# A transformer written anew: joined value and output weights, four column groups, feed-forward between tiles

## Chip, cores and metric

The kernel runs on one core of one Trainium2 chip. The metric is the device time of one execution in microseconds (us), the median of three runs.

## What is computed

The input x has the shape (2, 1024, 128): two sequences of 1024 tokens with 128 features. Six blocks follow one another, each with a residual: a windowed transformer of six layers, a recurrence over the tokens, the same transformer again (with the same weights), a mixture of 20 experts, full attention, and the mixture again. The change touches the two passes of the transformer alone. One of its layers, cut to what matters:

```
x = attn_layer(shift_tokens(x)) + x     # the last 64 features are taken from the token before
x = ffn_layer(shift_tokens(x)) + x

def attn_layer(x):                      # 16 heads of 64, Wqkv is 128 x 3072, Wo is 1024 x 128
    q, k, v = split(x @ Wqkv)
    q = rotary(l2norm(q) * qs); k = rotary(l2norm(k) * ksc)
    # windows of 32 tokens; each sees itself and the window before it (64 keys, a band mask)
    attn = softmax(mask(8 * q @ k.T)); out = attn @ v
    return out @ Wo

def ffn_layer(x):                       # 341 hidden features
    a, gate = split((layernorm(x) * g + b_ln) @ W1 + b1)
    return (a * gelu(gate)) @ W2 + b2
```

## The kernel before

Everything is float32. The activations lie in SBUF with features on the partitions (`c.xA`, `c.xB`); a tile is 128 tokens of one sequence, so that a layer has 16 tiles. `transformer` normalises x, and then runs `layer_phase` six times in a loop of the hardware (`nc.Fori`). `layer_phase` holds the programs of the five engines, which meet only at semaphores. Its tiles go through a hand-written pipeline of four stages, one tile of each sequence in turn: `project` (Q and K projection, L451), `turn` (rotated and normalised Q and K transposed, L413), `attend` (scores, softmax, values), `finish` (output projection and residual). Two tiles are in the loop body of `run`; the first and last tiles stand outside it, and behind the last one come the four groups of the feed-forward, 512 tokens each (`FeedForward`), after which the next layer starts.

What each engine does for one tile:

- TensorE projects Q and K (4 matmuls of 512 columns, L451), projects V for each of the four windows with its 64 keys (2 matmuls of 512 columns, one for the even and one for the odd heads, which write to partitions 0 to 63 and 64 to 127, L475), transposes Q and K (16 transposes, L413), the probabilities (8, L484) and the output (8, L440), adds the mask and forms scores (64 matmuls of 64 columns that read 64 partitions, L431), multiplies probabilities and values (64 of the same shape, L400), and projects the output with Wo (8 matmuls, L459). A matmul in float32 is two instructions in the trace, a transpose is one.
- VectorE rotates Q and K (L515, L523), sums squares (L555), takes the reciprocal square root in twelve small steps (`rsqrt_steps`, L92 to L98), takes each head's maximum (L538), subtracts it (L543), sums the exponentials (L567), and scales the output by the reciprocal sum (L593).
- ScalarE squares (L634), takes one exponential over all 16 heads (L627), and copies from PSUM: Q and K (L669), values (L643), probabilities (L647), the turned output (L623). In the feed-forward it does the scaling (L871) and Gelu (L881). Each layer loads the table of Exp (L670) and that of Gelu (L650) once.
- GpSimd adds the two rotated products (L371), scales them by the norm (L376), and makes shifted copies of x (L349, L352).

The queue of SyncE loads the next layer's weights when the last tile of a layer is done. The order in each engine's queue is fixed by the text of `stages`; an instruction that waits holds up all that stand behind it on its engine.

## Time and profile before

| | us |
|---|---|
| median of three runs | 7947.51 (7939.41 to 7956.17) |
| span of the profiled execution | 7947.7 |
| first transformer, first table load to the addition of its result | 2265.8 |
| second transformer, the same | 2269.9 |
| one layer (second layer to third) | 378.37 |
| one tile in the middle of a layer | 19.72 |
| TensorE, VectorE, ScalarE, GpSimd busy over the span | 6508.3, 5680.7, 2813.2, 1991.7 |

The span runs from the first to the last instruction of one execution on the chip. "Busy" is the time in which an engine executes; a wait on a semaphore is idle time. The mean length of a matmul (mean ns) contains the time that it spends in the array, so starts matter more than lengths: from one start to the next the trace tells how fast TensorE goes. PEld is the loading of the stationary operand, which can run beside matmuls. A granted clock of 1.00 is 2.4 GHz, one of 0.50 is 1.2 GHz.

### The profile page before, as it was taken

The page shows a single profiled execution, that of the slowest core. Times are in us where ns is not written, and L with a number is a line of the kernel's source. Part 1 is how long each engine was busy: PE and PEld are TensorE (multiplying, and loading weights), DVE is VectorE, ACT ScalarE, POOL GpSimd, SP SyncE. Part 2 cuts the span into 40 slices and gives each one's busy share as a digit, 9 for nine tenths or more (in the row PEclk, how much of TensorE's full clock was granted, in tenths as well). Part 3 has the DMA queues.
Part 4 walks back from the last instruction along what each step waited for, and adds up shares of the span by engine and source line. Part 5 has one row for each costly group of instructions (what it writes and reads, how often), then busy time and mean ns, then how long its engine had stood idle before and what let it go on. Part 6 is the DMA issues. An engine that isn't in the chain of part 4 may idle for free. (4 is left out here: it accounts for less than half of the span.)

```text
span 7947.7 us, 238408 instructions
## 1 busy us (share of the span) xinstructions
PE 6508.3 (82%) x89716; PEld 4710.8 (59%) x89716; DVE 5680.7 (71%) x26551; ACT 2813.2 (35%) x7328; POOL 1991.7 (25%) x2075
## 2 busy tenths in 40 slices
PE   8999999999976666666666666679999999999887
PEld 5656656565656565655656565656565655656544
DVE  6676767676767777777777777777666676767566
ACT  4444444444432222222222222234444444444311
POOL 4343535353510000000000000034444353535200
PEclk9999999999975555555555555589999999999898
DMA  0000000000000000000000000000000000000000
GB/s 28 11 4 14 1 14 1 14 1 14 1 15 2 2 2 2 2 2 2 2 2 2 2 2 2 2 4 0 15 11 4 11 4 14 1 14 1 18 2 12
DMA packets 30765, 50.49 MB, mean 6 GB/s; under 512 B 2032, under 2 KB 25291, under 8 KB 28235
## 3 DMA queue, kind: packets, MB, share of 16 engines
q1 hardware_dynamic: 29614, 40.54, 1.6%
q8 instruction: 425, 6.96, 0.4%
q14 instruction: 314, 2.56, 0.1%
q10 hardware_dynamic: 412, 0.42, 0.0%
HBM read 39.91 MB, written 1.05 MB: 5 GB/s over the span
## 5 line engine op out<-in xcount | busy, mean ns | idle before, releaser
L1048 PE MATMUL g_bank<-hbuf,Wgates 128*128 128x2 f32 x2048 | 600.9, 363 | 1024.2 <-DVE hbuf L1136 970.3
L1048 PEld LDWEIGHTS g_bank<-hbuf,Wgates 128*128 128x128 f32 x2048 | 513.0, 311 | 1140.0 <-DVE hbuf L1136 1085.3
L1090 ACT ACTIVATE tg<-g_bank 128x2 f32<-128x2 f32 x1024 | 176.1, 172 | 1690.9 <-PE g_bank L1048 1690.9
L1156 POOL TENSOR_TENSOR xB<-hbuf,xA 128x32 f32 x64 | 16.4, 256 | 2853.0 <-DVE hbuf L1136 2853.0
L371 POOL TENSOR_TENSOR t1b<-t1b,t2b 128x1024 f32<-128x1024 f32 x192 | 451.7, 2354 | 687.1 <-DVE t2b L523 687.1
L371 POOL TENSOR_TENSOR t1a<-t1a,t2a 128x1024 f32<-128x1024 f32 x192 | 451.7, 2354 | 684.7 <-DVE t2a L523 684.7
L1060 PE MATMUL e_bank<-tg,Weg 128*128 128x2 f32 x2048 | 579.4, 352 | 0.0
L1032 PEld LDWEIGHTS s_bank<-hparts,Wparts 128*128 128x128 bf16 x12288 | 571.0, 117 | 0.0
L1110 DVE TENSOR_SCALAR sg<-es 128x4 f32<-128x4 f32 x1024 | 174.4, 170 | 554.5 <-ACT es L1092 554.5
L1060 PEld LDWEIGHTS e_bank<-tg,Weg 128*128 128x128 f32 x2048 | 515.1, 312 | 0.0
L1032 PE MATMUL s_bank<-hparts,Wparts 128*128 128x2 bf16 x12288 | 469.6, 165 | 0.0
L555 DVE TENSOR_REDUCE ssqb<-sqb 128x16 f32<-128x1024 f32 x192 | 232.7, 1215 | 187.5 <-ACT sqb L634 187.5
L376 POOL TENSOR_TENSOR t1b<-t1b,rnormb 128x1024 f32<-128x1024 f32 x192 | 361.1, 1902 | 11.6 <-DVE rnormb L98 11.6
L376 POOL TENSOR_TENSOR t1a<-t1a,rnorma 128x1024 f32<-128x1024 f32 x192 | 361.0, 1901 | 11.6 <-DVE rnorma L98 11.6
L555 DVE TENSOR_REDUCE ssqa<-sqa 128x16 f32<-128x1024 f32 x192 | 232.5, 1215 | 182.3 <-ACT sqa L634 182.3
L1127 DVE SCALAR_TENSOR_TENSOR no<-ex,iso,fno 128x1 f32<-128x1 f32 x2048 | 352.0, 213 | 3.6 <-issue 1.7
L1146 DVE SCALAR_TENSOR_TENSOR cn<-ex,sg,fcn 128x1 f32<-128x1 f32 x2048 | 351.8, 214 | 0.0
L431 PEld LDWEIGHTS banksa<-KT,QTa 64*32 64x32 f32 x12288 | 292.1, 107 | 41.0 <-issue 41.0
L431 PEld LDWEIGHTS banksb<-KT,QTb 64*32 64x32 f32 x12288 | 292.1, 107 | 40.7 <-issue 40.7
L643 ACT COPY Vwb<-banksb 128x512 f32<-128x512 f32 x384 | 224.8, 586 | 256.5 <-PE banksb L475 256.1
L643 ACT COPY Vwa<-banksa 128x512 f32<-128x512 f32 x384 | 224.7, 586 | 255.9 <-PE banksa L475 255.5
L431 PE MATMUL banksa<-KT,QTa 64*32 64x64 f32 x12288 | 308.3, 218 | 0.0
(435 smaller groups left out, 16401.7 us busy)
## 6 DMA issues: line engine op xcount, KB each, us to landing
Wqkv<-in_L_ffn_Wqkv SPq DMA_DIRECT2D x13, 1536.0 KB, 6.5
Wo<-in_L_ffn_Wo SPq DMA_DIRECT2D x13, 512.0 KB, 7.6
W<-in_L_ffn_W SPq DMA_DIRECT2D x12, 341.0 KB
W<-in_L_ffn_W SPq DMA_DIRECT2D x12, 128.0 KB
xt<-in_L_attn_x SPq DMA_DIRECT2D x2, 512.0 KB
rope<-in_rope SPq DMA_DIRECT2D x1, 1024.0 KB, 7.5
out<-ot SPq DMA_DIRECT2D x4, 256.0 KB
W<-in_L_ffn_W SPq DMA_DIRECT2D x12, 42.5 KB
```

The lines of the kernel that those rows point to most:

```text
L371: pool.tensor_tensor(t1[:, part], t1[:, part], t2[:, part], ALU.add).then_inc(s.rot_sum, 1)
L376: pool.tensor_tensor(qview(t1[:, part]), qview(t1[:, part]), c.rnorm[:, i * HEADS:(i + 1) * HEADS].unsqueeze(2).to_broadcast([P, HEADS, DH ...
L431: last = pe.matmul(sc[WIN * w:WIN * w + WIN, col:col + KEYS], c.QT[rows, pair, WIN * w:WIN * w + WIN], c.KT[b][rows, pair, WIN * w:WIN * w ...
L555: dve.tensor_reduce(c.ssq[:, i * HEADS:(i + 1) * HEADS], qview(sq[:, i * INNER:(i + 1) * INNER]), AX.X, ALU.add).then_inc(s.ssq_done, 1)
L643: act.copy(c.Vw[:, w, :], vo[:, bank * 512:(bank + 1) * 512]).then_inc(s.v_ready, 1)
L1032: last = pe.matmul(out, Wparts[:, gate, w_part, :], hparts[:, h_part, :], start=False, stop=(w_part, h_part) == LAST_TERM, skip_group_chec ...
L1048: pe.matmul(g_bank[j][:, s * B:(s + 1) * B], Wg[:, 3, 1, :], h, start=False, stop=True, skip_group_check=True).then_inc(g_done, 1)
L1060: pe.matmul(e_bank[j][:, s * B:(s + 1) * B], Weg[:, :], tg[:, :], start=False, stop=True, skip_group_check=True).then_inc(e_done, 1)
L1090: act.activation(tg[:, :], g_bank[j][:, s * B:(s + 1) * B], ACT.Tanh).then_inc(tg_ready, 1)
L1110: dve.tensor_scalar(sg[:, :, :], es[:, :, :], 1.0, None, ALU.add).then_inc(sg_done, 1)
L1127: last = dve.scalar_tensor_tensor(out=no[:, b:b + 1], in0=ex[:, b:b + 1], scalar=iso[:, b:b + 1], in1=fno[:, b:b + 1], op0=ALU.mult, op1=A ...
L1146: last = dve.scalar_tensor_tensor(out=cn[:, 1, b:b + 1], in0=ex[:, b:b + 1], scalar=sg[:, 0, b:b + 1], in1=fcn[:, 1, b:b + 1], op0=ALU.mul ...
```

## The change

`layer_phase` and `FeedForward` go. Each pass of the transformer becomes one straight program of 96 tiles (six layers of 16) and six further steps, without loops of the hardware. Tiles now run through one sequence and then the other. In step i the engines work on tile `new` = i (projection of Q, then of K), tile `now` = i-1 (transposes, scores, exponentials), tile `old` = i-2 (values, transposed probabilities) and tile `last` = i-3 (probabilities times values, residual). In it:

- Wv and Wo are multiplied once a layer, head by head, into a 128 x 128 matrix for each head (`turn_weights`, `join_weights`; `take_weights` and `keep_weights` copy them from PSUM). This is done in steps 6 to 11 of the layer before. Values then have 128 features for each head, the output projection and the transposes of the output go, and one transpose of 128 x 128 is left (`turn_output`).
- Values are formed once for each window of 32 tokens, by four matmuls of 512 columns with 32 stationary columns, to four groups of 32 partitions. The probabilities are laid out so that 4 heads of 32 keys fill the 128 partitions; `attend` has 32 matmuls of 128 columns.
- K is stored block-diagonally (`KT` holds two heads side by side, with zeros between them), so that 32 score matmuls of 128 columns that read all 128 partitions take the place of 64. ScalarE fills it in four copies, one for each half and parity (`take_k`); GpSimd moves the last window (`move_k`).
- The exponential is taken head by head: 16 ACTIVATEs of 64 columns, with the negated maximum as bias, each of which also gives its sum (`accum_out`). VectorE's subtraction and its sum go; it only inverts the sums, and GpSimd multiplies the probabilities by them (`norm_probs`, two instructions of 512 columns).
- The Q and K projections share two banks of PSUM, K's after Q's, and the scores, the turned Q and the turned K share two. Values, turned probabilities and the weight products share one bank (`vp`), each waiting until ScalarE has copied the one before.
- The feed-forward works on groups of two tiles (256 columns) and is spread over the steps: `rows` in an even step, `back` and `gates` with `gelu` in the odd one after it, `lins`, `multiply`, `contract` and `finish` in the next even one.
- The rotary tables of the next layer are multiplied by GpSimd in steps 8 to 11; weights have two buffers and are no longer loaded in `load_phase`. At the start GpSimd clears `KT` (2 x 2560 columns) and `Vw` (4096 columns).

VectorE's order in a step is: `rotate_q(new)`, `squares_q(new)`, `residual(last)`, in even steps `multiply`, then `rotate_k(new)`, `largest(now)`, in even steps `finish`, then `squares_k(new)`, `norms(new)`, `invert(now)`, and in even steps `normalise` (statistics, reciprocal square root and scaling of a group). GpSimd's is: `move_k(now)`, `add_q(new)`, in even steps `shift_rows`, then `shift(new + 1)`, `add_k(new)`, `norm_q(new)`, `norm_k(new)`, `norm_probs(now)`.

```diff
                 sp.dma_start(maskf[:, :, :], d["mask"]).then_inc(mask_in, 16)
                 sp.dma_start(c.rope[:, :, :, :], d["rope"]).then_inc(rest_in, 16)
-                sp.dma_start(c.Wqkv[:, :], d["L0_ffn_Wqkv"][0]).then_inc(rest_in, 16)
-                sp.dma_start(c.Wo[:, :, :], d["L0_ffn_Wo"][0].rearrange("(j p) n -> p j n", p=P)).then_inc(rest_in, 16)
-                sp.wait_ge(rest_in, 16 * 5)
+                sp.wait_ge(rest_in, 16 * 3)
...
-def layer_phase(nc, c, layer, nm):
...
-class FeedForward:
...
+def tensor_program(pe, c, s, N):
...
+    def project_q(n):
+        layer = tile_place(n)[0]
+        pe.wait_ge(s.weights_in[layer % 2], 16 * (layer // 2 + 1))
+        pe.wait_ge(s.xq_ready, 2 * n + 2)
+        if n:
+            pe.wait_ge(s.k_prod, 2 * n)
+        for h in range(2):
+            last = pe.matmul(qk[h], c.xq[n % 4][:, :], c.Wqk[layer % 2][:, h * 512:(h + 1) * 512], start=True, stop=True)
+        last.then_inc(s.q_done, 1)
...
+    def turn_q(n):
+        pe.wait_ge(s.q_scaled, n + 1)
+        if n:
+            pe.wait_ge(s.exp_done, n)
+        for half in range(2):
+            for k in range(half * HALF, (half + 1) * HALF):
+                last = pe.transpose(sc[:, k * P:(k + 1) * P], t1[:, k * P:(k + 1) * P], c.ident[:, :])
+            last.then_inc(s.q_turned, 1)
...
+    def score(n):
+        layer, b, t = tile_place(n)
+        pe.wait_ge(s.kt_ready, 4 * n + 4)
+        pe.wait_ge(s.k_moved, 2 * n + 2)
+        for h in range(2):
+            pe.matmul(sc[:, h * 512:(h + 1) * 512], c.identb[:, :], c.mask[:, t, :].unsqueeze(1).to_broadcast([P, 8, KEYS]),
+                      start=True, stop=False, skip_group_check=True)
+        for pair in range(PAIRS):
+            for w in range(NW):
+                last = pe.matmul(sc[WIN * w:WIN * w + WIN, pair * 2 * KEYS:(pair + 1) * 2 * KEYS],
+                                 c.QT[:, pair, WIN * w:WIN * w + WIN],
+                                 c.KT[n % 2][:, pair, :, WIN * w:WIN * w + KEYS],
+                                 start=False, stop=True, skip_group_check=True)
+        last.then_inc(s.scored, 1)
...
+    def values(n, w):
+        layer = tile_place(n)[0]
+        pe.wait_ge(s.wvo_ready, 4 * (layer + 1))
+        if w == 0 and n:
+            pe.wait_ge(s.v_ready, 4 * n)
+            before, j = divmod(n + 1, TILES)
+            if before + 1 < N // TILES and 6 <= j < 8:
+                pe.wait_ge(s.wv_ready, 2 * (before + 1) + j - 5)
+            if before + 1 < N // TILES and 8 <= j < 12:
+                pe.wait_ge(s.wvo_ready, 4 * (before + 1) + j - 7)
+        if w == 1 or w == 3:
+            pe.wait_ge(s.v_ready, 4 * n + w)
+        if w == 2:
+            pe.wait_ge(s.pt_ready, 2 * n + 2)
+        for hq in range(4):
+            last = pe.matmul(vp[WIN * hq:WIN * hq + WIN, :], c.xq[n % 4][:, WIN * w:WIN * w + WIN], c.Wvo[layer % 2][:, hq, :],
+                             start=True, stop=True)
+        last.then_inc(s.v_done, 1)
...
+    def turn_probs(n, pc):
+        pe.wait_ge(s.p_scaled, 2 * n + pc + 1)
+        if pc == 0:
+            pe.wait_ge(s.v_ready, 4 * n + 2)
+        else:
+            pe.wait_ge(s.pt_ready, 2 * n + 1)
+        for quad in range(QUADS):
+            last = pe.transpose(vp[:, quad * P:(quad + 1) * P], c.probs[n % 2][:, quad, pc, :, :].rearrange("p h j -> p (h j)"),
+                                c.ident[:, :])
+        last.then_inc(s.p_turned, 1)
...
+    def attend(n):
+        pe.wait_ge(s.v_ready, 4 * n + 4)
+        pe.wait_ge(s.pt_ready, 2 * n + 2)
+        if n:
+            pe.wait_ge(s.x_done, n)
+        first = NW * (n % 2)
+        for pc in range(2):
+            for quad in range(QUADS):
+                for w in range(NW):
+                    slot = (first + w - 1 + pc) % (2 * NW)
+                    last = pe.matmul(o[WIN * w:WIN * w + WIN, 0:P], c.PT[:, pc, quad * P + WIN * w:quad * P + WIN * w + WIN],
+                                     c.Vw[:, slot, quad * P:(quad + 1) * P],
+                                     start=(pc == 0 and quad == 0), stop=(pc == 1 and quad == QUADS - 1), skip_group_check=True)
+        last.then_inc(s.pv_done, 1)
...
+    for i in range(N + 6):
+        new, now, old, last = i, i - 1, i - 2, i - 3
+        even, g = i % 2 == 0, (i - 4) // 2
+        layer, j = divmod(i, TILES)
+        if new < N:
+            project_q(new)
+        if 0 <= now < N:
+            turn_q(now)
+        if 0 <= last < N:
+            attend(last)
+        if 0 <= old < N:
+            values(old, 0)
+        if 0 <= now < N:
+            turn_k(now)
+        if 0 <= last < N:
+            turn_output(last)
+        if 0 <= old < N:
+            values(old, 1)
+        if even and 0 <= g - 1 < G:
+            lins(g - 1)
+        if not even and 0 <= g < G:
+            back(g)
+        if new < N:
+            project_k(new)
+        if 0 <= old < N:
+            turn_probs(old, 0)
+        if 0 <= now < N:
+            score(now)
+        if 0 <= old < N:
+            turn_probs(old, 1)
+            values(old, 2)
+        if even and 0 <= g - 1 < G:
+            contract(g - 1)
+        if not even and 0 <= g < G:
+            gates(g)
+        if 0 <= old < N:
+            values(old, 3)
+        if even and 0 <= g < G:
+            rows(g)
+        if layer + 1 < N // TILES and 6 <= j < 12:
+            pe.wait_ge(s.v_ready, 4 * (old + 1))
+            if j < 8:
+                turn_weights(layer + 1, j - 6)
+            else:
+                join_weights(layer + 1, j - 8)
+def vector_program(dve, c, s, N):
...
+    def largest(n):
+        dve.wait_ge(s.scored, n + 1)
+        if n:
+            dve.wait_ge(s.exp_done, n)
+        dve.tensor_reduce(c.mx[:, :], sc.rearrange("p (h j) -> p h j", j=KEYS), AX.X, ALU.max).then_inc(s.max_done, 1)
+        dve.wait_ge(s.max_done, n + 1)
+        dve.tensor_scalar(c.mx[:, :], c.mx[:, :], -1.0, None, ALU.mult).then_inc(s.negated, 1)
+    def invert(n):
+        dve.wait_ge(s.exp_done, n + 1)
+        if n >= 2:
+            dve.wait_ge(s.p_scaled, 2 * (n - 1))
+        dve.reciprocal(c.rinv[n % 2][:, :], c.rsum[n % 2][:, :]).then_inc(s.inverted, 1)
+def scalar_program(act, c, s, N):
...
+    def take_k(n):
+        act.wait_ge(s.k_moved, 2 * n + 2)
+        for half in range(2):
+            act.wait_ge(s.k_turned, 2 * n + half + 1)
+            for par in range(2):
+                rows = slice(64 * par, 64 * par + 64)
+                act.copy(c.KT[n % 2][rows, half * HALF:(half + 1) * HALF, par, WIN:],
+                         sc[rows, half * 512:(half + 1) * 512].rearrange("p (k m) -> p k m", m=P)).then_inc(s.kt_ready, 1)
+    def exponent(n):
+        act.wait_ge(s.negated, n + 1)
+        if n >= 2:
+            act.wait_ge(s.p_turned, 2 * (n - 1))
+            act.wait_ge(s.inverted, n - 1)
+        for h in range(HEADS):
+            last = act.activation(c.probs[n % 2][:, h // 4, :, h % 4, :], sc[:, h * KEYS:(h + 1) * KEYS].rearrange("p (a j) -> p a j", a=2), ACT.Exp, bias=c.mx[:, h:h + 1],
+                                  accum_out=c.rsum[n % 2][:, h:h + 1])
+        last.then_inc(s.exp_done, 1)
+    def take_values(n, w):
+        act.wait_ge(s.v_done, 4 * n + w + 1)
+        if n:
+            act.wait_ge(s.pv_done, n)
+        act.copy(c.Vw[:, NW * (n % 2) + w, :], vp).then_inc(s.v_ready, 1)
...
+    for i in range(N + 6):
+        new, now, old, last = i, i - 1, i - 2, i - 3
+        even, g = i % 2 == 0, (i - 4) // 2
+        layer, j = divmod(i, TILES)
+        if new < N:
+            square_q(new)
+        if 0 <= now < N:
+            take_q(now)
+        if 0 <= last < N:
+            take_output(last)
+        if 0 <= old < N:
+            take_values(old, 0)
+        if 0 <= now < N:
+            take_k(now)
+        if 0 <= old < N:
+            take_values(old, 1)
+        if not even and 0 <= g < G:
+            scale(g)
+        if new < N:
+            square_k(new)
+        if 0 <= old < N:
+            take_probs(old, 0)
+            take_probs(old, 1)
+            take_values(old, 2)
+        if 0 <= now < N:
+            exponent(now)
+        if 0 <= old < N:
+            take_values(old, 3)
+        if layer + 1 < N // TILES and 6 <= j < 12:
+            if j < 8:
+                take_weights(layer + 1, j - 6)
+            else:
+                keep_weights(layer + 1, j - 8)
+        if not even and 0 <= g < G:
+            gelu(g)
+def pool_program(pool, c, s, N):
...
+    def norm_probs(n):
+        pool.wait_ge(s.inverted, n + 1)
+        for pc in range(2):
+            pr = c.probs[n % 2][:, :, pc, :, :]
+            pool.tensor_tensor(pr, pr, c.rinv[n % 2][:, :].rearrange("p (q h) -> p q h", h=4).unsqueeze(3).to_broadcast([P, QUADS, 4, WIN]),
+                               ALU.mult).then_inc(s.p_scaled, 1)
```

## Rows read from the trace of the kernel before

**Rows 1.** The page: busy time of each engine over the whole span.
```profile
PE 6508.3 (82%) x89716; PEld 4710.8 (59%) x89716; DVE 5680.7 (71%) x26551; ACT 2813.2 (35%) x7328; POOL 1991.7 (25%) x2075
```

**Rows 2.** Table by stretches; columns: stretch, length, each engine busy, granted clock, DMA share, GB/s.
```profile
34.91:2300.74 2265.83, 2146.71 (x32304) 1385.90 (x32304) 1573.32 (x2875) 1018.51 (x1548) 979.84 (x972) 0.98 0.03 8
5229.00:7498.91 2269.91, 2151.10 (x32304) 1388.42 (x32304) 1575.22 (x2874) 1019.11 (x1548) 979.66 (x972) 0.98 0.02 8
639.45:659.17 19.72, 19.72 (x333) 13.31 (x331) 14.49 (x25) 9.74 (x15) 9.83 (x11) 1.00 0.00 0
413.35:791.72 378.37, 357.94 (x5384) 231.09 (x5385) 262.32 (x480) 169.91 (x258) 163.13 (x162) 0.98 0.03 8
2600.00:2800.00 200.00, 125.93 (x1633) 117.67 (x1630) 150.54 (x1335) 47.84 (x284) 1.01 (x4) 0.50 0.01 2
```

**Rows 3.** Timeline of TensorE where the second layer starts.
```profile
413.35 6.02 PE L451 MATMUL banksa<-Wqkv,xq0a 128*128 128x512 f32 x8 [5.23 <-issue]
```

**Rows 4.** Timeline of one tile; columns: start, length, engine, line, operation, operands, count.
```profile
639.45 3.60 PE L451 MATMUL banksa<-Wqkv,xq0a 128*128 128x512 f32 x8
...
647.22 1.08 PE L475 MATMUL banksa<-Wqkv,xs0a 128*64 128x512 f32 x4
...
648.23 0.42 PEld L484 LDWEIGHTS banksa<-ident,probsa 128*128 128x128 f32 x4 [0.81 <-issue]
...
648.35 0.59 ACT L643 COPY Vwa<-banksa 128x512 f32<-128x512 f32 x1 [0.43 <-PE banksa L475]
...
649.83 1.09 PE L413 MATMUL banksa<-ident,t1a 128*128 128x128 f32 x8
...
655.11 3.21 PE L431 MATMUL banksa<-KT,QTa 64*32 64x64 f32 x128
...
658.24 0.86 PEld L440 LDWEIGHTS banksa<-ident,Ona 128*128 128x128 f32 x8
...
659.17 3.60 PE L451 MATMUL banksa<-Wqkv,xq1a 128*128 128x512 f32 x8
```

**Rows 5.** Groups by line and shape from 600 to 1400 us: count, busy us, mean ns.
```profile
L371 POOL TENSOR_TENSOR t1a<-t1a,t2a 128x1024 f32<-128x1024 f32 x68 | 160.0, 2354 | 243.0 <-DVE t2a L523 243.0
...
L376 POOL TENSOR_TENSOR t1a<-t1a,rnorma 128x1024 f32<-128x1024 f32 x70 | 131.6, 1902 | 3.9 <-DVE rnorma L98 3.9
...
L515 DVE TENSOR_TENSOR t1a<-banksa,rla 128x1024 f32<-128x1024 f32 x68 | 83.2, 1224 | 32.2 <-PE banksa L413 25.2 <-ACT sqa L634 6.2
...
L643 ACT COPY Vwa<-banksa 128x512 f32<-128x512 f32 x136 | 79.6, 586 | 91.2 <-PE banksa L475 91.0
...
L634 ACT ACTIVATE sqa<-banksa 128x1024 f32<-128x1024 f32 x70 | 67.9, 1013 | 34.2 <-PE banksa L451 34.2
...
L881 ACT ACTIVATE fga<-banksa,lcolsa 128x512 f32<-128x512 f32 x16 | 11.0, 688 | 32.8 <-PE banksa L770 28.7 <-DVE fha L836 4.1
...
L349 POOL COPY xq1a<-xA 64x128 f32 x13 | 3.7, 287 | 4.6 <-POOL fxsa L352 4.6
```

**Rows 6.** Timeline of VectorE: first step of a reciprocal square root and the step behind it.
```profile
24.57 0.17 DVE L92 TENSOR_SCALAR anvar<-anvar 128x16 f32<-128x16 f32 x1
...
27.08 5.19 DVE L285 TENSOR_SCALAR anxn<-antok,anmv,anrstd 128x128 f32<-128x128 f32 x16
```

**Rows 7.** Timeline of ScalarE in full attention (first two) and at a change of function table.
```profile
7686.15 1.11 ACT L1508 ACTIVATE apr<-a_banks,amx 128x1024 f32<-128x1024 f32 x1 [3.95 <-DVE amx L1480]
7687.17 0.19 ACT L1508 ACTIVATION_READ_ACCUMULATOR apr<-a_banks,amx 128x1 f32 x1
...
367.60 1.28 ACT L650 ACT_TABLE_LOAD   x1
368.89 0.20 ACT L650 ACTIVATE scrap<-ones 128x1 f32<-128x1 f32 x1
369.00 0.76 ACT L871 ACTIVATE fxnTa<-banksa,lcolsa 128x512 f32<-128x512 f32 x1
```

**Rows 8.** Timeline of TensorE in full attention.
```profile
7716.09 1.97 PE L1448 MATMUL a_banks<-ident,apr 128*128 128x128 f32 x8 [1.57 <-DVE apr L1488]
```

**Rows 9.** Table by stretches of the same us, columns as in rows 2.
```profile
7716.00:7717.00 1.00, 0.91 (x4) 0.91 (x5) 0.86 (x3) 0.00 (x0) 0.00 (x0) 0.50 0.00 0
```

968 lines of the change are left out of this document (439 added, 529 removed).

## The prediction

> **What bounds the kernel now.** I read the page's busy times first, and then the table by stretches, for an average over the span hides the stages. TensorE is busiest over the whole [rows 1]; inside a tile of a transformer it is busy for all of the 19.72 us, at the full clock, beside VectorE 14.5, ScalarE 9.7 and GpSimd 9.8 [rows 2]. Sixteen such tiles are 315.5 us of a layer's 378.4, so 63 us of each layer are filling and draining the pipeline, a feed-forward by itself, and a restart with a 5.2 us pause after which the projection goes at half speed (6.02 us against 3.60) [rows 2, 3, 4]. The two transformers take 2265.8 + 2269.9 = 4535.7 us [rows 2], 23.6 us for each tile. The rest of the span, 7947.7 - 4535.7 = 3412.0 us, is not touched. The median of the runs is 0.2 us below the span; I forecast for both alike.
>
> **Prices.** TensorE, by starts: a 512-column float32 matmul is two instructions of 0.43 us (eight end after 3.60, some 0.2 of it the last one's stay in the array), so two of 256 columns 0.21, of 128 columns 0.107; a transpose 0.108 (the loads of eight in 0.86); the 128 small score instructions take 3.13 us up to the next load, 0.0245 each, though 64 columns alone would be 0.053: instructions in different parts of the array overlap [rows 4]. Four instructions of 512 columns to two column groups let the next load start after 1.01 us, where 1.71 would be serial [rows 4]: two groups do run together. A result reaches ScalarE 1.13 us after the start of such a set [rows 4], that is 0.27 after its last issue. ScalarE: a copy of 512 columns lasts 0.59, a square of 1024 1.01, hence 0.83 ns a column; back to back they start 0.49 and 0.92 apart, as about 0.1 overlaps. Gelu of 256 columns: 0.69 - 0.21 = 0.48, apart 0.38. VectorE: 1.22 for 1024 columns, 1.14 apart; twelve steps 2.5 us [rows 5, 6]. GpSimd: 2.35, 1.90, small copies 0.3 with 0.25 between [rows 5].
>
> **What goes, what comes, by engine.** TensorE for a tile: Q and K 3.4, 25 transposes 2.7, mask 0.4, scores and attend 64 instructions of 0.107 each over four groups, 1.7 + 1.7, values 32 instructions over four groups 3.4, feed-forward half of (4 x 0.108 + 18 x 0.213) = 2.1, joined weights 4.3 a layer, 0.3: 15.8 against 19.7. Four groups together are not in the trace; bounds are serial (four times) and the overlap of two that is seen; I take four, for the small scores already go faster than two parts allow. VectorE: rotations 4.6, sums and maximum 3.5, norms 2.6, small ones 0.8, feed-forward half of 6: 14.5. GpSimd: 8.5, plus 1.9 for the probabilities, some 3 of moves and shifts: 13.4.
>
> ScalarE gets most. Twelve copies of 512 columns 5.9, squares 1.8, output 0.2, half of four feed-forward ACTIVATEs 0.8. Exp and Gelu alternate every second tile, so two tables for two tiles: 1.3 a tile by the 1.28 us row [rows 7]. In the trace the read of the accumulator is an instruction of its own, 0.19 us, starting 1.02 after an ACTIVATE of 1024 columns; 960 columns less put it 0.22 after one of 64, which itself lasts 1.11 - 0.80 = 0.31 [rows 7]. A 0.20 us ACTIVATE on one column lets the next start after 0.11 [rows 7]. So one head costs 0.33 (all overlaps) to 0.50 (none), 16 heads 5.3 to 8.0 us, where one Exp now takes 1.06 of a tile. I take 0.36, near the low end, since every other pair on ScalarE overlaps: 5.8. Sum: 15.8. No engine fills 20 us, so the chain decides.
>
> **The chain.** Q's turn, K's turn, scores and exponential use one pair of banks, so `turn_q` of the next tile waits for the last of 16 heads. I count from there, in us. Even step: ScalarE copies the last values 0.6, loads Gelu's table to 1.9, three Gelus 3.0, `square_q` 3.9, Q copies 4.9, output and first values 5.6, K's copies 7.5 (TensorE's `turn_q`, `attend`, `values` fit beside). TensorE: second values 5.7 to 6.6, `lins` 7.9, `project_k` 9.6 (it stands behind them in the queue), probabilities 10.0, mask and scores 12.2, second probabilities 12.6. They arrive at 12.9, copied 13.5; one bank, so `values` w=2 only now, 14.65, copied 15.2; Exp's table 16.5; heads 22.3. VectorE's maximum is ready at 14.6. Beside it `contract` delays `finish` and the norms to 20.3, and GpSimd's `norm_q` ends at 22.2: nearly level, so a cheaper exponential would gain next to nothing here.
>
> Odd step: VectorE inverts and only then runs `normalise`, 0.3 to 4.6; `rotate_q` waits behind it, to 6.9; `project_k` 8.7, scores 11.2, second probabilities arrive 11.9, copied 12.5, values 13.7, copied 14.3, heads 20.1. Mean of both 21.2. Changes between full and divided array cost 0.1 to 0.2 in the trace between the transposes and the next stage [rows 4]; three on the chain, 0.4. Clock: after its last early projection TensorE pauses 3 to 4 us under the heads. In full attention a 1.57 us wait after little work preceded eight transposes in 1.97 us instead of 1.09, at a granted 0.50 [rows 4, 8, 9]. Each such fall costs about 1.5 us of TensorE, but `turn_q` and `attend` have that slack beside ScalarE and `normalise`; 0.2. Together T = 21.8 us.
>
> **Steps 6 to 11.** TensorE waits for the last copy of values (0.55), makes a quarter of the joined weights (0.4 to 0.9) and then only projects the next Q (1.7), which elsewhere hides under the heads; ScalarE copies 0.6 more. Of 3 us some is slack: 2.5 each, 30 of them in a pass: 75 (40 to 100).
>
> **Ends of a pass.** Before the first projection: weights, clearing 9216 columns on GpSimd, joined weights: 18 us. The first three steps save 13; the six drain steps (19, 11, 6, 7, 5, 1) cost 49: 54 in all (30 to 80). The five restarts and the pauses between layers are gone, as the next layer's first tiles need only groups that ended steps ago.
>
> **Sum.** A pass: 96 x 21.8 + 75 + 54 = 2222; twice, plus 3412: 7856 us, 1.2% faster. It breaks even at T = (2267.9 - 129)/96 = 22.3. The removed 63 us a layer and the slower tile nearly cancel.
>
> A rule against it: on two tables in turn, the Trainium skill (ScalarE: Activation LUTs, What ACT_TABLE_LOAD costs) gives about 1.28 us for the load and 1.38 for a drain, and advises batching by set. By the rule T would be 23.2 and the time 8125. The trace agrees on 1.28, yet the instruction after the load starts 1.29 after it and the load right behind the copy before [rows 7]: no drain is seen, so I keep 1.28. Another rule: the Trainium skill (TensorE: Matmul & The Clock Gate, Part 3) lets weight loads overlap running matmuls only in other row groups. The new matmuls all read 128 rows; the row of two column groups above reads 128 rows too and overlaps, against the rule.
>
> **Rivals.**
> - *Each head costs 0.50* (14%). The read waits for the ACTIVATE and the next ACTIVATE for the read. Place: `exponent`, in the chain of every step. T = 21.8 + 16 x 0.14 = 24.1, time 8300, slower. It decides from 0.39 a head on, by 16 x (h - 0.36) = 0.5. For it: dependence through one accumulator. Against: the read starts before its ACTIVATE ends.
> - *The four column groups overlap only in twos* (9%), so that part of the change does not do what it says. Scores, `attend` and values double; on the chain 4.6 in either step: T = 26.4, 8740. For it: two is all that is shown. All in one row would add 1.7 more to each of scores and `attend` and is in this case's chance; it is what the rule of the Trainium skill (TensorE: Matmul & The Clock Gate, Part 3) comes to.
> - *The clock stays low for much of each tile* (12%), as in the recurrence, which has it at 0.50 with TensorE 63% busy [rows 2]. A fall's 1.5 us not hidden: T = 23.3, 8145.
> - *Each table load costs as much again* (4%), an emptying engine beside the 1.28 us: T = 21.8 + 1.28 = 23.1, 8105; or a dozen hand-overs cost 0.1 us more each, the same time (4%). The first is where the Trainium skill's drain (ScalarE: Activation LUTs, What ACT_TABLE_LOAD costs) would lead.
> - *Things that I put in a row overlap* (15%): VectorE and GpSimd run ahead, T = 20, near the busiest engine's 16 plus waits: 2 x (1920 + 129) + 3412 = 7510; halfway 7680.
> - The forecast as worked (42%): its own range, T 21.2 to 22.4, is 7740 to 7970.
>
> **How the numbers follow.** The likeliest is 7855. The slow cases hold 43% with 8105 to 8740. For the range I cut the widest (two column groups) and the far end of the fast one, for 2 in 10: 7600 to 8320. A difference under 0.2% (16 us) can't be told from none. Faster: 15% plus nine tenths of 42%: 0.53; within 0.2%: 0.04; slower: 43%.
>
> **What would show it.** In the profile after: a tile every 21.8 us, even steps about 2 longer; ScalarE busiest in a tile, with 1536 reads of the accumulator a pass; ACTIVATE starts of the heads 0.36 apart; `turn_q` released by ScalarE; no pause at layer starts; 96 table loads over both passes for each function; values in four groups with 0.86 us between sets. Wrong would be: heads 0.5 apart, values sets of 1.7, or a granted clock well under 0.9 through the tiles. VectorE or GpSimd releasing `turn_q` would mean that the norms' chain is longer than mine.

## The result, and the profile after

The changed kernel takes 8123.7 us (median of 4 runs, 8122.6 to 8127.9) beside 7945.4 us for the kernel before on the same chip: ratio 1.0224, 95% interval 1.0209 to 1.0238. It is slower, where the forecast was 7855 and faster. The range (7600 to 8320) holds the time.

The page of the changed kernel, its span, its busy times and the row of the granted clock:

```profile
PE 5985.7 (74%) x65140; PEld 4146.4 (51%) x65140; DVE 5702.2 (70%) x27235; ACT 3845.9 (47%) x13898; POOL 2436.5 (30%) x2297
...
PEclk9999999999975555555555555579999999999898
```

The table by stretches: the first pass, the second pass, and of the first pass the time from the first `norm_q` to the last and the time behind the last.

```profile
32.56:2385.17 2352.61, 1883.88 (x20016) 1101.80 (x20016) 1586.24 (x3217) 1535.21 (x4833) 1201.95 (x1083) 0.93 0.03 8
5308.00:7666.00 2358.00, 1887.48 (x20020) 1106.68 (x20020) 1585.97 (x3217) 1536.18 (x4835) 1202.09 (x1083) 0.92 0.03 8
...
74.60:2318.60 2244.00, 1818.19 (x19551) 1063.03 (x19551) 1559.70 (x3141) 1502.97 (x4751) 1173.23 (x1058) 0.93 0.02 6
2318.60:2385.17 66.57, 44.06 (x413) 26.72 (x413) 16.18 (x58) 25.65 (x75) 10.15 (x12) 0.79 0.00 1
```

The second stretch is taken a little wide: by the same marks as the first, from GpSimd's clearing of `KT` to the addition of the result, the second pass is 5310.36 to 7665.53. Against [rows 2] the passes grew from 2265.8 and 2269.9 to 2352.6 and 2355.2 us, together 172 us, and the rest of the span is what it was (8120.8 - 4707.8 = 3413 us). TensorE's work did shrink, 2146.7 to 1883.9 us a pass; the time did not follow, since no engine fills a step. ScalarE, 1018.5 before, has 1535.2.

The step between two tiles is read from the starts of GpSimd's `norm_q`. Three of them in the changed kernel:

```profile
491.62 1.90 POOL L909 TENSOR_TENSOR t1a<-t1a,rnorma 128x1024 f32<-128x1024 f32 x1 [5.17 <-DVE rnorma L91]
514.39 1.90 POOL L909 TENSOR_TENSOR t1a<-t1a,rnorma 128x1024 f32<-128x1024 f32 x1 [3.97 <-DVE rnorma L91]
538.31 1.90 POOL L909 TENSOR_TENSOR t1a<-t1a,rnorma 128x1024 f32<-128x1024 f32 x1 [5.18 <-DVE rnorma L91]
```

Undisturbed odd steps take 22.76 us and even ones 22.26 (45.0 for the pair), some even ones 23.92 like the second distance here. A step counts as odd or even by its number i: its length is the distance from the `norm_q` of step i-1 to that of step i. The steps with weights take 24 to 26. A whole layer is 382 us.

TensorE's timeline at the hand-over to an even step (first line, after the 16 heads of the odd step before it) and to an odd one:

```profile
808.93 1.09 PE L389 MATMUL banksa<-ident,t1a 128*128 128x128 f32 x8 [2.66 <-POOL t1a L909]
...
831.19 1.69 PE L389 MATMUL banksa<-ident,t1a 128*128 128x128 f32 x8 [3.34 <-POOL t1a L909]
```

`turn_q` is released by GpSimd's `norm_q`, not by the heads, in both. That is the sign that the prediction gave for "the norms' chain is longer than mine". ScalarE's timeline of the same place, the first heads and what follows the last:

```profile
802.72 0.32 ACT L763 ACTIVATE probs0a<-banksa,mxa 128x64 f32<-128x64 f32 x1 [0.20 <-DVE mxa L643]
802.93 0.19 ACT L763 ACTIVATION_READ_ACCUMULATOR probs0a<-banksa,mxa 128x1 f32 x1
803.02 0.31 ACT L763 ACTIVATE probs0a<-banksa,mxa 128x64 f32<-128x64 f32 x1
...
807.36 0.68 ACT L771 COPY Vwa<-banksa 128x512 f32<-128x512 f32 x1
808.06 1.28 ACT L813 ACT_TABLE_LOAD   x1
809.36 1.19 ACT L813 ACTIVATE fga<-banksa,cols 128x256 f32<-128x256 f32 x3
810.44 1.02 ACT L732 ACTIVATE sqa<-banksa 128x1024 f32<-128x1024 f32 x1
811.35 1.07 ACT L745 COPY QTa<-banksa 128x512 f32<-128x512 f32 x2
```

A head every 0.29 us, 16 in 4.65 us: cheaper than the 0.36 and 5.8 us of the forecast. So ScalarE was overpriced, and the time still came out longer. VectorE's timeline says why. The first lines are of an odd step, the rest of the end of an even one:

```profile
800.06 1.21 DVE L641 TENSOR_REDUCE mxa<-banksa 128x16 f32<-128x1024 f32 x1
801.31 1.37 DVE L643 TENSOR_SCALAR mxa<-mxa 128x16 f32<-128x16 f32 x1
802.60 1.21 DVE L627 TENSOR_REDUCE ssqa<-sqa 128x16 f32<-128x1024 f32 x1
804.25 0.18 DVE L85 TENSOR_SCALAR ssqa<-ssqa 128x32 f32<-128x32 f32 x1 [0.45 <-issue]
...
831.01 0.17 DVE L667 COPY fvara<-fmva 128x2 f32<-128x2 f32 x1
831.21 1.81 DVE L85 TENSOR_SCALAR fvara<-fvara 128x2 f32<-128x2 f32 x1
833.05 0.97 DVE L86 TENSOR_SCALAR frstda<-fvara 128x2 int32<-128x2 int32 x1
834.06 1.22 DVE L87 TENSOR_SCALAR frstda<-frstda 128x2 int32<-128x2 int32 x1
835.31 0.16 DVE L89 TENSOR_TENSOR ftmpa<-frstda 128x2 f32<-128x2 f32 x1
```

GpSimd's timeline of the same two places:

```profile
800.29 2.36 POOL L904 TENSOR_TENSOR t1a<-t1a,t2a 128x1024 f32<-128x1024 f32 x1 [2.55 <-DVE t2a L602]
...
831.10 1.90 POOL L914 TENSOR_TENSOR t1a<-t1a,rnorma 128x1024 f32<-128x1024 f32 x1
832.96 2.05 POOL L921 TENSOR_TENSOR probs1a<-probs1a,rinv1a 128x512 f32<-128x512 f32 x2
834.95 0.67 POOL L893 MEMSET KT0a<- 64x256 f32 x2
```

Two columns for each partition take 1.81 us here, and the same operation on 32 columns 0.18 us, with GpSimd idle. The slow ones end within 0.03 us of the end of an instruction of GpSimd: the negation L643 at 802.68, `add_k` L904 at 802.65; L85 at 833.02, `norm_k` L914 at 833.00; L86 at 834.02, the first `norm_probs` at 834.01. L87 ends at 835.28, 0.27 behind the second `norm_probs` (835.01) and with the first clearing of `move_k` (834.95 + 0.31); where a copy follows in place of the clearing, it ends with the second `norm_probs` and lasts 0.97 us. This isn't rare: over both passes 190 of the 192 negations and 276 of the 288 operations of the first three lines of `normalise` last over 0.7 us. The Trainium skill (SBUF — State Buffer, Who interferes with whom) has this as an exclusive lock on a port pair that VectorE and GpSimd share: VectorE's copies and `tensor_scalar` can take it in their two-port modes, and an instruction with at most one input in SBUF, outside these modes, does not contend. The rows agree with the lock, and the second experiment tests what an input in PSUM changes.

### The profile page after: what moved, and what is told of

Its sections match the earlier page's. It is cut to its first block and busy times, and to the rows that moved or that the text cites. A ratio compares the mean times of both kernels' runs of the same rounds, so it can differ in the third digit from the quotient of the medians.

```text
span 8120.8 us, 187306 instructions
## 1 busy us (share of the span) xinstructions
PE 5985.7 (74%) x65140; PEld 4146.4 (51%) x65140; DVE 5702.2 (70%) x27235; ACT 3845.9 (47%) x13898; POOL 2436.5 (30%) x2297
## 3 DMA queue, kind: packets, MB, share of 16 engines
HBM read 37.81 MB, written 1.05 MB: 5 GB/s over the span
## 5 line engine op out<-in xcount | busy, mean ns | idle before, releaser
L1257 POOL TENSOR_TENSOR xB<-hbuf,xA 128x32 f32 x64 | 16.5, 258 | 2850.2 <-DVE hbuf L1237 2850.2
L904 POOL TENSOR_TENSOR t1b<-t1b,t2b 128x1024 f32<-128x1024 f32 x96 | 226.5, 2359 | 365.2 <-DVE t2b L602 365.2
L904 POOL TENSOR_TENSOR t1a<-t1a,t2a 128x1024 f32<-128x1024 f32 x96 | 226.5, 2359 | 364.9 <-DVE t2a L602 364.9
L1200 ACT ACTIVATE ex<-e_bank 128x2 f32<-128x2 f32 x1024 | 176.4, 172 | 324.7 <-PE e_bank L1161 324.7
L909 POOL TENSOR_TENSOR t1a<-t1a,rnorma 128x1024 f32<-128x1024 f32 x96 | 182.5, 1902 | 434.9 <-DVE rnorma L91 434.9
L909 POOL TENSOR_TENSOR t1b<-t1b,rnormb 128x1024 f32<-128x1024 f32 x96 | 182.6, 1902 | 433.8 <-DVE rnormb L91 433.8
L1133 PE MATMUL o_bank<-hparts,Wparts 128*128 128x2 bf16 x6144 | 305.5, 165 | 0.0
L600 DVE TENSOR_TENSOR t1b<-banksb,rl0b 128x1024 f32<-128x1024 f32 x96 | 117.4, 1223 | 243.5 <-ACT sqb L738 104.8
```

The costliest lines, as they stand in the source:

```text
L904: pool.tensor_tensor(t1[:, INNER:], t1[:, INNER:], t2[:, INNER:], ALU.add).then_inc(s.k_sum, 1)
L909: pool.tensor_tensor(heads(t1[:, 0:INNER]), heads(t1[:, 0:INNER]), c.rnorm[:, 0:HEADS].unsqueeze(2).to_broadcast([P, HEADS, DH]), ALU.mult ...
L1133: last = pe.matmul(out, Wparts[:, gate, w_part, :], hparts[:, h_part, :], start=False, stop=(w_part, h_part) == LAST_TERM, skip_group_chec ...
L1200: act.activation(ex[:, :], e_bank[j][:, s * B:(s + 1) * B], ACT.Exp).then_inc(ex_ready, 1)
```

## The experiments

All changes are to the changed kernel (8123.7 us); ratios are to the kernel before, which ran between 7942.9 and 7950.1 us (medians) beside them. The differences in us compare chips, and that spread of 7 us is their uncertainty. Theory: the step is set by the chain from VectorE's norms to `norm_q`, lengthened where GpSimd holds up VectorE's small operations. Rival: the heads and ScalarE set it, as the forecast's chain had it.

**No negation.**

```diff
-        dve.tensor_reduce(c.mx[:, :], sc.rearrange("p (h j) -> p h j", j=KEYS), AX.X, ALU.max).then_inc(s.max_done, 1)
-        dve.wait_ge(s.max_done, n + 1)
-        dve.tensor_scalar(c.mx[:, :], c.mx[:, :], -1.0, None, ALU.mult).then_inc(s.negated, 1)
+        dve.tensor_reduce(c.mx[:, :], sc.rearrange("p (h j) -> p h j", j=KEYS), AX.X, ALU.max, negate=True).then_inc(s.negated, 1)
```

> The maximum is written with its sign turned by the reduction itself, and the 128x16 negation behind it (1.37 us, ended by the end of GpSimd's add_k) is gone. Theory, the chain through VectorE's norms and GpSimd's norm_q sets the step and VectorE's small operations are held up by GpSimd: odd steps lose 1.3 us (squares_k and the norms start that much earlier), even steps about nothing, since finish behind it waits for the contraction, which ends 0.7 us after the negation already; 94 odd steps x 1.3 = 120 us, so about 8000. Rival, the 16 heads and ScalarE set the step: the exponential also starts 1.3 us earlier in odd steps, and in even steps too where the Exp table is in by then (it is not: the table's load ends 1.2 us after the negation), so it too gives about 8000, but turn_q would then be released by ScalarE.

Measured 7992.0 us (ratio 1.0056, 1.0039 to 1.0073): 132 less, about the forecast 120. But the steps show another way to it. Odd steps fell to 21.38, by 1.38 as expected, and even ones rose to 23.06, by 0.8. TensorE's and VectorE's timelines of such an even step:

```profile
456.45 1.06 PE L389 MATMUL banksa<-ident,t1a 128*128 128x128 f32 x8 [1.13 <-ACT probs0a L761]
459.22 1.04 PE L431 MATMUL banksa<-Wvo1a,xq0a 128*32 128x512 f32 x8
460.81 1.06 PE L397 MATMUL banksa<-ident,t1a 128*128 128x128 f32 x8 [0.55 <-ACT QTa L743]
```

```profile
469.59 1.21 DVE L641 TENSOR_REDUCE mxa<-banksa 128x16 f32<-128x1024 f32 x1
472.93 0.48 DVE L691 SCALAR_TENSOR_TENSOR xA<-banksa,cols,xB 128x256 f32<-128x256 f32 x1 [2.13 <-PE banksa L527]
```

At this hand-over `turn_q` is released by the heads now, which is the rival's sign, and the copies of Q wait behind the Gelu table and the Gelus; at the other it still waits for `norm_q` (3.33 us). A pair of steps gained only 0.6 us: so near was ScalarE's chain behind. And in even steps `finish` waits 2.13 us for the contraction instead of 0.72, so the negation's time went into a wait, as expected. The rest of the 132 us is in the steps with weights and the falls of the clock.

**The negation kept, its input in PSUM.**

```diff
-        dve.tensor_reduce(c.mx[:, :], sc.rearrange("p (h j) -> p h j", j=KEYS), AX.X, ALU.max).then_inc(s.max_done, 1)
+        most = o[:, 256:256 + HEADS]
+        dve.tensor_reduce(most, sc.rearrange("p (h j) -> p h j", j=KEYS), AX.X, ALU.max).then_inc(s.max_done, 1)
         dve.wait_ge(s.max_done, n + 1)
-        dve.tensor_scalar(c.mx[:, :], c.mx[:, :], -1.0, None, ALU.mult).then_inc(s.negated, 1)
+        dve.tensor_scalar(c.mx[:, :], most, -1.0, None, ALU.mult).then_inc(s.negated, 1)
```

> Nothing is left out: the maximum is written to PSUM (columns of bank 3 that nothing uses), and the same negation reads it there and writes SBUF as before. If GpSimd's running add holds up an operation of VectorE only where it reads and writes SBUF, the negation takes 0.1 to 0.3 us instead of 1.37 and the time is within 20 us of that without a negation (about 8010). If the negation is slow of itself, or if it waits for the maximum's result to arrive, it keeps 1.3 us and the time stays at 8124.

Measured 8006.5 us (1.0072, 1.0056 to 1.0089). The groups by tile, of the changed kernel and of this one; the three numbers are the shortest, median and longest in ns:

```profile
L643 DVE TENSOR_SCALAR mxa<-mxa x34: 1367/1371/1375, 601.7 to 1390.8; 128x16 f32<-128x16 f32 x34
```

```profile
L644 DVE TENSOR_SCALAR mxa<-banksa x34: 174/175/176, 611.8 to 1389.3; 128x16 f32<-128x16 f32 x34
```

The same operation, at the same place behind the same maximum, 1371 ns from SBUF and 175 ns from PSUM, with GpSimd's `add_k` running beside it in either kernel. That GpSimd holds it up through SBUF is shown, and it alone costs 117 us.

**`finish` behind the norms.**

```diff
             largest(now)
-        if even and 0 <= g - 1 < G:
-            finish(g - 1)
         if new < N:
             squares_k(new)
             norms(new)
+        if even and 0 <= g - 1 < G:
+            finish(g - 1)
```

> finish of the feed-forward (waits for the contraction, 0.72 us idle and 0.48 us busy in even steps) stands behind squares_k and the norms on VectorE; the rest is as it was. Theory of the norms' chain: even steps lose 1.1 us, from the negation's end straight to squares_k, odd steps nothing: 92 even steps x 1.1 = 100 us, so about 8025. Rival, heads and ScalarE: the heads' start and end don't move, 8124.

Measured 8037.5 us (1.0115, 1.0098 to 1.0132): 86 less for 100 expected. Even steps are 21.05 and odd ones 23.16, a pair 0.8 shorter. The rival had nothing here.

**`normalise` in the next step's gap.**

VectorE's part of the edit:

```diff
             residual(last)
+        if not even and 0 <= g < G:
+            normalise(g)
...
             invert(now)
-        if even and 0 <= g < G:
-            normalise(g)
```

`back` moves behind `score` on TensorE and `scale` between the copies of the two halves of the probabilities on ScalarE.

> normalise stands behind rotate_q, squares_q and the residual of the next step instead of ahead of them; back follows behind the scores on TensorE and scale behind the first probabilities' copy on ScalarE. Theory: rotate_q starts at the end of square_q, about 5 us earlier in odd steps, project_k no longer waits its 1.0 us, and normalise lies in the time in which VectorE waits for square_k; what is left behind is TensorE's own order, so 0.7 to 1.0 us less in each odd step, 65 to 95 us, about 8045. Below 7950 would mean that the fall of the clock in the pause goes away with it. Rival, heads and ScalarE: nothing, 8124. Rival, normalise is held up by GpSimd's add_q just as by its norm_k in its new place and rotate_k waits for it: same or slower, up to 8200.

Measured 8039.1 us (1.0119, 1.0102 to 1.0136): 85 less, inside the expected 65 to 95. Its odd steps are 21.55 and its even ones 22.26 as before.

**A cheap exponential.**

```diff
-        dve.reciprocal(c.rinv[n % 2][:, :], c.rsum[n % 2][:, :]).then_inc(s.inverted, 1)
+        dve.reciprocal(c.rinv[n % 2][:, :], c.mx[:, :]).then_inc(s.inverted, 1)
...
-        for h in range(HEADS):
-            last = act.activation(c.probs[n % 2][:, h // 4, :, h % 4, :], sc[:, h * KEYS:(h + 1) * KEYS].rearrange("p (a j) -> p a j", a=2), ACT.Exp, bias=c.mx[:, h:h + 1],
-                                  accum_out=c.rsum[n % 2][:, h:h + 1])
+        for h in range(0, HEADS, 4):
+            last = act.activation(c.probs[n % 2][:, h // 4, :, :, :], sc[:, h * KEYS:(h + 4) * KEYS].rearrange("p (h a j) -> p a h j", a=2, h=4),
+                                  ACT.Exp, bias=c.mx[:, h:h + 1])
```

The kernel leaves out the sums and twelve of the sixteen maxima.

> The exponential is left coarse: one ACTIVATE for four heads with the first head's maximum and no sums, four in all instead of 16, and the inverse is taken of the maxima, so the probabilities are not normalised. The heads' 4.65 us become about 1.3 us. Theory of the norms' chain: turn_q doesn't wait for the exponential, so only invert and normalise come earlier, by 0.8 to 1.0 us in odd steps, and normalise's small operations are held up by GpSimd all the same until it has finished: 0 to 1.0 us in each odd step, 8030 to 8124. Rival, the heads and ScalarE set the step: 3.3 us less in each of 190 steps, about 7500.

Measured 7974.8 us (1.0033, 1.0021 to 1.0044), 149 less. That is more than my theory's 0 to 94 us, though far from the rival's 620. The starts of `norm_q` show where it lies:

```profile
503.72 1.90 POOL L909 TENSOR_TENSOR t1a<-t1a,rnorma 128x1024 f32<-128x1024 f32 x1 [3.96 <-DVE rnorma L91]
525.98 1.90 POOL L909 TENSOR_TENSOR t1a<-t1a,rnorma 128x1024 f32<-128x1024 f32 x1 [5.18 <-DVE rnorma L91]
548.74 1.90 POOL L909 TENSOR_TENSOR t1a<-t1a,rnorma 128x1024 f32<-128x1024 f32 x1 [3.97 <-DVE rnorma L91]
```

22.26 and 22.76, as with 16 heads: 3.3 us less of ScalarE in each step leaves ordinary steps where they were. Nearly all of the gain is in the steps with weights (in the second layer 25.6, 25.4, 26.1, 25.1, 26.3, 24.3 became 22.3, 25.3, 22.3, 25.3, 22.3, 22.8), because a piece of the weights waits there for the copy behind the heads. I had left that out of the expectation. TensorE's timeline of such a step in the changed kernel:

```profile
584.71 1.11 PE L475 MATMUL banksa<-ident,Wva 128*128 128x128 f32 x4 [4.47 <-ACT Vwa L771]
585.62 3.62 PE L373 MATMUL banksa<-Wqk1a,xq3a 128*128 128x512 f32 x4
589.03 1.12 PE L389 MATMUL banksa<-ident,t1a 128*128 128x128 f32 x8
```

TensorE is idle for 4.47 us, and then `project_q`, which elsewhere lies under the heads, goes at half speed (3.62 us against 1.88) straight ahead of `turn_q`.

**The weights' pieces behind `turn_q`.**

```diff
             turn_q(now)
+        if layer + 1 < N // TILES and 7 <= j < 13:
+            pe.wait_ge(s.v_ready, 4 * (last + 1))
+            if j < 9:
+                turn_weights(layer + 1, j - 7)
+            else:
+                join_weights(layer + 1, j - 9)
...
```

The same lines go from the end of TensorE's step, and on ScalarE the copies move likewise from the end of the step to behind `take_q`.

> The transposition and joining of the next layer's weights, one piece in each of steps 6 to 11, stand behind turn_q of the next step on TensorE and behind the copies of Q on ScalarE, instead of at the end of the step ahead of project_q. Now a piece waits for the copy behind the 16 heads, holds back project_q and with it turn_q, and costs about 3 us a step; in the new place its 1.0 us lies in TensorE's row of work and the attention covers its copy: 1.0 to 1.3 us a step. 60 such steps x 1.8 us = 110 us less, about 8015. Rival, the surplus of these steps is TensorE's and ScalarE's work itself, wherever it stands: no change, 8124.

Measured 8049.6 us (1.0124, 1.0107 to 1.0141), 74 less where 110 was expected. The pieces follow `turn_q` at once, but in every second of these steps TensorE has just been idle 3.3 us for `norm_q`, and a step of 26.6 us is left: the attention takes 3.64 us there and 1.95 elsewhere, at a granted clock that has fallen to 0.50.

**No normalising of the probabilities.**

```diff
-            pr = c.probs[n % 2][:, :, pc, :, :]
-            pool.tensor_tensor(pr, pr, c.rinv[n % 2][:, :].rearrange("p (q h) -> p q h", h=4).unsqueeze(3).to_broadcast([P, QUADS, 4, WIN]),
-                               ALU.mult).then_inc(s.p_scaled, 1)
+            pr = c.probs[n % 2][:, 0, pc, 0, 0:2]
+            pool.tensor_tensor(pr, pr, c.rinv[n % 2][:, 0:2], ALU.mult).then_inc(s.p_scaled, 1)
```

The kernel leaves out the normalising but for two elements in each half.

> GpSimd's normalising of the probabilities is left out but for two elements in each half (2 x 2.05 us of GpSimd time become about 0.2), so the output is not normalised. Theory, GpSimd's running instructions hold up normalise's small operations in odd steps: of L85 1.81, L86 0.97 and L87 1.22 us the last two fall to 0.2, normalise ends 1.8 us earlier and project_k no longer waits its 1.0 us: 0.8 to 1.2 us in each odd step, about 8030, and nothing in even steps. Rival, the probabilities' path (invert, normalising, their transposition) sets the step: its transposition comes 8 us after it, so this can't be seen here; rival, GpSimd is only busy beside VectorE and holds up nothing: L86 and L87 keep their durations and the time stays at 8124.

Measured 8029.7 us (1.0098, 1.0081 to 1.0115), 94 less, as expected; odd steps are 21.55 and even ones 22.26 as before. (The two `norm_probs` take 1.05 us each, 2.05 together, and not 2.05 each.) The groups of `normalise`'s first three small operations:

```profile
L85 DVE TENSOR_SCALAR fvara<-fvara x17: 1808/1816/1824, 627.4 to 1378.4; 128x2 f32<-128x2 f32 x17
L86 DVE TENSOR_SCALAR frstda<-fvara x17: 168/169/170, 629.3 to 1380.2; 128x2 int32<-128x2 int32 x17
...
L87 DVE TENSOR_SCALAR frstda<-frstda x17: 305/396/1528, 629.5 to 1380.4; 128x2 int32<-128x2 int32 x17
```

L86 fell from 0.97 to 0.17 us, and L85, under `norm_k`, kept its 1.8: each is held up by the very GpSimd instruction that runs beside it. L87 still meets the next one now and then.

**Four edits together** (no negation, `finish` and `normalise` moved, weights behind `turn_q`), nothing left out.

> Four edits together, nothing left out: the maximum negated by its own reduction, finish behind the norms, normalise behind the residual of the next step, and the weights' pieces behind turn_q. By the theory even steps lose 2.5 us (negation 1.3 and the wait for the contraction 1.1, which each hid behind the other), odd steps 1.3 + 0.9, the steps with weights 1.8 more: 92 x 2.5 + 94 x 2.2 + 60 x 1.8 = 545 us, 7580; but by then the 16 heads end level with norm_q in even steps and release turn_q, which takes back 0.5 us and more there: 7580 to 7700, below the 7945 of the kernel before. If the gains of the single edits only add up (-132, -86, -85 and what the weights give), it is 7710; if they hide each other, above that.

Measured 7564.7 us (0.9515, 0.9499 to 0.9531): 559 less, where the four alone add up to 377. It is even below the expected 7580 to 7700, which had taken something back for the heads. The step is 20.33 us, odd or even:

```profile
420.27 1.90 POOL L908 TENSOR_TENSOR t1a<-t1a,rnorma 128x1024 f32<-128x1024 f32 x1 [2.59 <-DVE rnorma L91]
440.60 1.90 POOL L908 TENSOR_TENSOR t1a<-t1a,rnorma 128x1024 f32<-128x1024 f32 x1 [2.58 <-DVE rnorma L91]
460.93 1.90 POOL L908 TENSOR_TENSOR t1a<-t1a,rnorma 128x1024 f32<-128x1024 f32 x1 [2.58 <-DVE rnorma L91]
```

and its granted clock over about one layer, the last but one number in the table of stretches, stands here ahead of the changed kernel's:

```profile
412.00:740.00 328.00, 280.76 (x3303) 163.43 (x3305) 211.12 (x502) 247.52 (x799) 196.39 (x177) 1.00 0.03 10
```

```profile
431.00:806.00 375.00, 305.93 (x3250) 178.72 (x3247) 262.65 (x530) 249.26 (x787) 192.50 (x174) 0.93 0.03 8
```

TensorE's pauses ahead of `turn_q` are 0.9 and 1.1 us here and the clock stays at 1.00; in the changed kernel they are 2.3 and 3.3 us, and it falls behind them again and again. What releases `turn_q` here, from its group:

```profile
L389 PE MATMUL banksa<-ident,t1a x304: 272/273/329, 612.2 to 1383.7; 128*128 128x128 f32 x152
...
  ACT probs1a L761: 16.2, 19
  POOL t1a L908: 13.8, 12
  ACT probs0a L761: 7.9, 7
```

In the changed kernel GpSimd alone stood in this list, with 56.8 us; now the heads have 24.1 of 37.9.

**The Exp table ahead of time**, added to the four: in even steps, behind `take_probs(old, 0)`,

```diff
+        if even and 0 <= now < N:
+            act.activation(c.scrap[:, :], c.ident[:, 0:1], ACT.Exp)
```

> The four edits of the run before, and in even steps an exponential of one column behind the first probabilities' copy, so that the Exp table's 1.28 us lie in ScalarE's idle time there. In the four-edit kernel turn_q of the next step was released by the last head (736.9) and norm_q had ended at 735.6. Theory, the heads bind in even steps by now: 1.2 us less in 92 to 95 steps, up to 115 us, about 7450. Rival, the norms' chain still binds: nothing, 7565.

Measured 7469.4 us (0.9393, 0.9377 to 0.9408), 95 less: the table's 1.28 us went into ScalarE's idle time. Steps are 19.56 and 20.06, and `turn_q`'s list is

```profile
  POOL t1a L910: 23.9, 18
  ACT probs0a L761: 2.2, 2
```

**Two of the four** (no negation, `finish` behind the norms).

> Only the negation folded in and finish behind the norms, of the four edits. By themselves they gave 132 and 86 us. Theory: in even steps the negation (1.3 us) hid behind finish's wait for the contraction, so removing both gives 2.5 us there and 1.3 in odd steps: 92 x 2.5 + 94 x 1.3 = 350 us, 7770, more than their sum. Rival, they only add up: 7905.

Measured 7877.6 us (0.9903, 0.9887 to 0.992): 246 less, more than 132 + 86 = 218, but not the 350 of the theory. A pair of steps lost 2.7 us (21.86 + 20.48) of the 3.8 that I gave it. The heads release `turn_q` at both hand-overs now: behind even steps they end 1.5 us after `norm_q`, behind odd ones 0.1 us. What else of ScalarE's order holds them was not tried by itself.

**The four, with the cheap exponential.**

> The four edits, with the coarse exponential (four ACTIVATEs, no sums, probabilities not normalised). On the changed kernel it gave nothing in ordinary steps (22.26 and 22.76 as before) and 149 us in the steps with weights, where the piece waited behind the heads' copy. Theory: with the norms' chain shorter the heads release turn_q, and it now gives 1.2 us and more in each pair of ordinary steps too: 60 us and more, 7400 to 7500, with the gain in the ordinary steps and not only in those with weights. Rival, the norms' chain still sets these steps: they stay at 20.33.

Measured 7382.6 us (0.9283, 0.9268 to 0.9299), 182 less than the four alone, a little more than expected. The pair of ordinary steps fell from 40.66 to 39.2 (19.56 and 19.66). The same edit that did nothing for ordinary steps of the changed kernel gains 1.4 us a pair here: whichever chain is longer hides what the other costs.

**`norm_q` in halves**, added to the early table.

```diff
+        for half in range(2):
+            part = t1[:, half * 512:(half + 1) * 512]
+            pool.tensor_tensor(heads(part), heads(part), c.rnorm[:, 8 * half:8 * half + 8].unsqueeze(2).to_broadcast([P, 8, DH]),
+                               ALU.mult).then_inc(s.q_scaled, 1)
...
```

`turn_q` waits for each half, and for the first eight heads and then the rest.

> The kernel with the early table, and norm_q in two halves of 512 columns, with turn_q's first four transpositions behind the first half and the first eight heads. Nothing is left out. TensorE can start 0.9 us earlier on the first half where norm_q releases it and 2.3 us where the heads do, but the second half still comes when it did, and the attention behind it waits for that: 0.5 us in each step at most, 0 to 95 us below the kernel with the early table. Rival: two operations on GpSimd cost 0.1 to 0.2 us more than one, and the whole is the same or slower by 20.

Measured 7476.8 us (0.9403, 0.9387 to 0.9419), 7 more than without: the rival. Steps 19.93 and 19.69, the same sum.

The kernel with the four edits and the early table computes everything and beats both, by 6.1% and 8.1%.

## Why the prediction was wrong, by its own steps

- **The chain, the step that failed.** The prediction has "`norm_q` ends at 22.2: nearly level" in the even step, and worked out no norms' chain in the odd one, whose 20.1 us went by the heads alone. From the end of the heads (807.36) the next ones ended at 22.5, where 22.3 was forecast, and `norm_q` at 23.8 (831.14), against 22.2; in ordinary steps of either kind `norm_q` ends some 1.0 us after the last head. In the odd step "`normalise`, 0.3 to 4.6" ended 7.6 after the heads, `rotate_q` 9.9 (forecast 6.9), `project_k` some 12 (8.7). The pair took 45.0 us against 42.4 before additions and 43.6 with them. The even step, 22.26, is about as long as its 22.3 before additions; the odd one is 22.76 and not 20.1, though even steps were to be the longer by 2. The durations of VectorE's small operations were taken as free of what GpSimd does: about 0.2 us each, where five in each pair of steps (two negations, three of `normalise`) waited 0.8 to 1.6 us for a GpSimd instruction. The waits of the three in `normalise`, 3.2 to 3.5 us together, account for the 3.0 us by which it ended late. The second and seventh runs show this; the negation alone is worth 117 to 132 us and `normalise`'s place or partner 85 to 94. No run frees all five and changes nothing else, so how much of the miss they make together stays open.
- **The heads.** Rightly put under 0.39, but 0.29 and not 0.36. "A cheaper exponential would gain next to nothing" was right of ordinary steps and wrong of those with weights.
- **Busy time of a tile**, a pass's over 96: VectorE 16.5 us (forecast 14.5), ScalarE 16.0 (15.8), GpSimd 12.5 (13.4), TensorE 19.6 (15.8, though its terms add up to 15.7). TensorE's was the worst, with the falls of the clock in it; the pauses of 2.3 and 3.3 us ahead of `turn_q` show that it still had room.
- **The sum.** A pass was to be 96 x 21.8 + 75 + 54 = 2222 and took 2352.6, 131 more. In it 95 steps took 2244.0; 95 x 21.8 + 75 is 2146: 98 more. A layer's 382.3 us, less 16 ordinary steps of 22.85 (the last layer's 342.8 over 15), leaves 16.6 for its six weight steps, against 15: that term was nearly right, though the runs show that most of it is a wait and not work. So 98 us of the 131 lie in the steps, nearly all of them in the ordinary step, 1.05 too short. The ends took 2352.6 - 2244.0 = 108.6 against 54 + 21.8 = 75.8: 33 more, with 66.6 behind the last `norm_q` at a clock of 0.79; they were not tried. 131 in the first pass, 133 in the second, and 3413 for 3412 are the whole miss of 265 us (8120.8 for 7856).
- **Clock.** 0.2 us a step was forecast. A fall behind the pause of 3.3 us, at the start of an odd step, is hidden (22.76 to 22.80 with it); one behind the pause of 2.3 us, at the start of an even step, makes that 23.92 instead of 22.26, once or twice in a layer's ordinary steps, 0.1 to 0.2 a step: about right. In the kernel of four edits, with pauses of 0.9 and 1.1 us, such steps are gone.
- **Column groups of four**, taken against the nearest row and a rule: right. A set of values, eight instructions of 512 columns, goes by in 1.00 us (next start), where 0.86 was forecast and one after the other they would take 3.4. **Table loads** at 1.28 us without a drain: right (808.06 to the Gelu's start at 809.36). So two of the slow rivals fell.
- **Rivals.** None named this mechanism. The sentence on what would show the forecast wrong named the longer norms' chain, and gave it no price. The trace of the kernel before doesn't show the price: in its first pass no `tensor_scalar` or copy of VectorE within SBUF took over 0.33 us, as none met more than a short copy or the end of a long instruction of GpSimd.

## What to carry to other kernels

Before pricing a chain, lay the small operations of VectorE beside GpSimd's timeline: here a `tensor_scalar` that read and wrote SBUF lasted until GpSimd's instruction ended, so put its input in PSUM, fold it into a reduction, or move it to where GpSimd is idle. When two chains are nearly level, work out both in every kind of step; single edits then can gain less than their size and together more than their sum (here 559 against 377 us). Do not put work that waits for the end of a chain ahead of what starts the next one, and load a table by a one-column operation in idle time.

## What the hardware showed that was not expected

- A `tensor_scalar` of two columns took up to 1.82 us beside GpSimd; one of 16 columns took 1371 ns from SBUF and 175 ns from PSUM.
- Three such operations in a row were held up by GpSimd's instructions in turn (1.81, 0.97, 1.22 us): the engines alternate, and GpSimd's next instruction starts before VectorE's next (832.96 and 833.05). The third lasted through two of GpSimd's, the second `norm_probs` and a clearing.
- An ACTIVATE of 64 columns with its read of the accumulator repeats every 0.29 us, though the two instructions show 0.3 and 0.2 us.
